# Cross attention's first keys, two blocks' queries and the first block's maxima made beside self attention's last pair of heads

## The reference, cut to what matters

```python
x = x + attn(layernorm(x))             # 16 heads of 16, causal, ALiBi
q = (layernorm(x) @ Wq + bq)           # cross attention: (2048, 16 heads, 64)
k = (ctx @ Wk + bk); v = (ctx @ Wv + bv)   # (1601, 16 heads, 64)
scores = einsum('bqhd,bkhd->bhqk', q, k) / 8
out = einsum('bhqk,bkhd->bqhd', softmax(scores), v) @ Wo + bo + layernorm(x)
x = x + layernorm(out) * gamma + beta
x = x + fp8_product(layernorm(x))
```

## Time and profile before

| | us |
|---|---|
| median of 3 runs | 1922.67 |
| lowest, highest | 1912.9, 1936.35 |
| profiled execution, its own time | 1929.99 |
| its span, first to last instruction | 1928.2 |
| PE busy, mean granted clock | 1758.9, 0.947 |
| DVE / ACT / POOL busy | 1289.3 / 921.8 / 974.3 |

### The profile page before, as it was taken

The page is one execution under the profiler, slowest core; times in us unless marked ns, Lnnn a source line. Parts: engine busy times, 40 slices in busy tenths (PEclk is TensorE's granted clock), DMA queues, the critical chain, the costliest instruction groups (busy, mean ns, idle before and its releaser), DMA issues.

```text
span 1928.2 us, 29741 instructions
## 1 busy us (share of the span) xinstructions
PE 1758.9 (91%) x10650; PEld 886.1 (46%) x10650; DVE 1289.3 (67%) x2503; ACT 921.8 (48%) x1866; POOL 974.3 (51%) x824
## 2 busy tenths in 40 slices
PE   7989988988998999999999999999999999999962
PEld 3544444434444544445545545545544554554421
DVE  5677777766733557756756655665665665678998
ACT  2346667656765243244444444445445445445531
POOL 1000000000001466558888888898898898882244
PEclk9879999889988899899999999999999999999985
DMA  4232311250011000000000000000000000000001
GB/s 115 35 36 36 35 18 19 36 98 2 1 47 42 11 0 1 1 11 4 1 10 4 1 10 4 1 11 1 4 10 1 4 1 1 4 11 23 1 28 38
DMA packets 29129, 34.48 MB, mean 18 GB/s; under 512 B 4290, under 2 KB 27139, under 8 KB 27523
## 3 DMA queue, kind: packets, MB, share of 16 engines
q1 hardware_dynamic: 28984, 32.59, 9.1%
HBM read 14.99 MB, written 4.19 MB: 10 GB/s over the span
## 4 chain that ended last, share of the span: by engine, by line
PE 76%; DVE 16%; issue 3%; ACT 3%; SPq 1%; POOL 1%; DMA 0%; POOLq 0%; ACTq 0%; DVEq 0%
PE psum L964 17%; PE psum L944 14%; PE psum L929 9%; DVE maxima L1229 8%; PE psum L850 7%; PE psum L762 6%; PE psum L800 4%; PE psum L825 4%; PE psum L987 3%; PE psum L917 3%; PE psum L862 2%; PE psum L975 2%; DVE parts_room L1323 1%; DVE stack_room L1279 1%; PE psum L877 1%
## 5 line engine op out<-in xcount | busy, mean ns | idle before, releaser
L1229 DVE TENSOR_REDUCE maxima<-psum 128x1 f32<-128x400 f32 (+5 forms) x1664 | 858.8, 578 | 315.2 <-PE psum L929 214.3
L737 POOL TENSOR_TENSOR parts_room<-parts_room,weights_room 128x512 f32<-128x512 f32 (+1 forms) x565 | 705.6, 1279 | 141.3 <-ACT weights_room L1119 141.3
L1119 ACT ACTIVATE weights_room<-psum 128x512 f32<-128x512 f32 (+1 forms) x757 | 405.8, 599 | 500.2 <-PE psum L944 423.4
L1047 ACT ACTIVATE weights_room<-psum 128x512 f32<-128x512 f32 (+3 forms) x640 | 300.1, 534 | 178.1 <-PE psum L825 99.5
L1436 POOL TENSOR_SCALAR rstd<-meanvar 128x2 f32<-128x2 f32 (+1 forms) x24 | 8.2, 343 | 650.7 <-DVE meanvar L1179 650.7
L944 PE MATMUL psum<-stack_room,dk_hi 64*128 64x512 f32 (+1 forms) x1408 | 264.5, 410 | 4.9 <-ACT weights_room L1119 4.8
L929 PE MATMUL psum<-k_later,stack_room 64*128 64x400 f32 (+1 forms) x896 | 243.6, 412 | 22.5 <-DVE stack_room L1279 14.6
L929 PEld LDWEIGHTS psum<-k_later,stack_room 64*128 64x128 f32 x896 | 129.0, 185 | 221.2 <-issue 121.9
L964 PE MATMUL psum<-weights_room,parts_room 128*64 128x512 f32 (+1 forms) x754 | 204.6, 610 | 0.0
L964 PE MATMUL psum<-weights_room,late_room 128*64 128x512 f32 (+1 forms) x760 | 203.9, 609 | 0.0
L825 PE MATMUL psum<-stack_room,stack_room 51*128 51x512 f32 (+3 forms) x640 | 140.1, 437 | 36.6 <-DVE maxima L1229 34.4
(11 more groups left out here) (133 smaller groups left out, 1907.7 us busy)
## 6 DMA issues: line engine op xcount, KB each, us to landing
stack_room<-parts_room SPq DMA_DIRECT2D x84, 128.0 KB
x_block<-x_dram SPq DMA_DIRECT2D x8, 512.0 KB, 4.7
x_middle<-x_block SPq DMA_DIRECT2D x4, 512.0 KB, 3.2
x_block<-x_middle SPq DMA_DIRECT2D x4, 512.0 KB, 3.8
out_dram<-x_block SPq DMA_DIRECT2D x8, 256.0 KB, 2.1
stack_room<-parts_room SPq DMA_DIRECT2D x24, 64.0 KB
parts_room<-ctx_dram SPq DMA_DIRECT2D x1, 1536.0 KB
stack_room<-shift_rows SPq DMA_DIRECT2D x64, 2.0 KB
```

The costliest lines, as they stand in the source:

```text
L737: engine.tensor_tensor(sum_[:kw, :], old[:kw, :], weights[u % NP_WEIGHTS][:kw, :], ALU.add) \
L1047: engine.activation(w_self[s % NW][:, m, 0:n], bank_of(use + m)[:, 0:n], ACT.Exp, scale=SELF_SCALE).then_inc(emptied(use + m), 1)
L1119: engine.activation(weights[u % NP_WEIGHTS][:kw, :], pair_scores[u % NSCORES][:kw, :], ACT.Exp, scale=CROSS_SCALE).then_inc(pair_exp, 1)
L1229: engine.tensor_reduce(maxima[:, p % 2, i // TB, n, i % TB, ch:ch + 1], bank_of(use + n)[:, 0:real - k0], AX.X, ALU.max) \
```

## The change

Pair 0's keys, without their rests, are made beside blocks 0 to 2 of self attention's last pair, and beside its block 3, from the tenth of its 24 steps on, the transposed residual of blocks 0 and 1, the queries of blocks 0 and 1, and the 16 chunks of block 0 with their negated maximum. `check_turned` asserts in the planner that self attention's block 2 has been turned by then. Only the rows and the key rests stand at `cross_start`. The residual and queries of blocks 2 and 3 and the residual's bias go beside block 0 of cross attention's second sweep, pair 1's keys and queries from beside block 0 to beside block 1. The waits follow: ACT's copies of keys and queries no longer wait for the end of self attention, those of the rests now do; the pads of the keys' buffers are cleared ahead of the last pair; `shifts` gets another place, and the first keys one in the room of the ALiBi table.

```diff
--- before.py
+++ after.py
@@ -173,7 +173,12 @@ class Order
     def self_turn(self, b):
         for c in range(DC):
             self.put("self_turn", b, c, banks=1)
+        self.turned = b
         self.after(OUT_LAG, lambda: self.self_out(b))
+
+    def check_turned(self, b):
+
+        assert self.turned >= b
...
-    def pair_sweep1(self, p, blocks=range(NB), waits=False):
+    def pair_sweep1(self, p, blocks=range(NB), waits=False, rows=True):
...
             made.append((len(steps) + ROWS_LAG, lambda b=b: self.put("pair_rows", p, b, banks=1)))
+        if not rows:
+            return steps
...
-    def pair_keys(self, p):
+    def pair_keys(self, p, rests=True):
         steps = []
         for b in range(NK):
             steps.append((1, lambda b=b: self.put("project_keys", p, b, banks=1)))
+            if not rests:
+                steps.append((0, lambda b=b: self.put("key_steps", p, b)))
+                continue
...
+    def resid_turn(self, b):
+        return [(1, lambda c=c: self.put("resid_turn", b, c, banks=1)) for c in range(DC)]
...
@@ -372,25 +385,31 @@ def build
             else:
-                self.interleave(self.sweep2(p), [])
+
+
+                main = self.sweep2(p)
+                last = [n for n, m in enumerate(main) if m[2] == NB - 1]
+                put("key_pads")
+                self.spread(main[:last[0]], self.pair_keys(0, rests=False), range(TB, last[0]))
+                queries = self.pair_queries(0)
+                early = self.resid_turn(0) + queries[:1] \
+                    + self.mingled(self.pair_sweep1(0, [0], rows=False), self.resid_turn(1) + queries[1:2])
+                self.spread(main[last[0]:], [(0, lambda: self.check_turned(HT))] + early, range(9, len(last)))
         while self.pending or self.soon:
             self.values()
 
-        def now(steps):
-            for _, step in steps:
-                step()
-
+        put("pair_rows", 0, 0, banks=1)
         put("cross_start")
         self.step = 0
-        now(self.pair_keys(0))
-        for b in range(NB):
-            for c in range(DC):
-                put("resid_turn", b, c, banks=1)
-        put("resid_bias")
-        now(self.pair_queries(0) + self.pair_sweep1(0, [0], waits=True))
-
-        sides = [self.pair_tiles(0) + self.pair_sweep1(0, [1]) + self.pair_keys(1) + self.pair_queries(1),
-                 self.pair_sweep1(0, [2]) + self.pair_sweep1(1, [0]), self.pair_sweep1(0, [3]) + self.pair_sweep1(1, [1]),
+        for b in range(NK):
+            put("key_rests", 0, b)
+        late = [step for b in range(HT, NB) for step in self.resid_turn(b)] + queries[HT:] \
+            + [(0, lambda: put("resid_bias"))]
+
+        rows = [(0, lambda: put("pair_rows", 0, 1, banks=1))]
+        sides = [self.pair_tiles(0) + self.pair_sweep1(0, [1], rows=False) + late[:HT] + rows + late[HT:],
+                 self.pair_sweep1(0, [2]) + self.pair_keys(1) + self.pair_queries(1) + self.pair_sweep1(1, [0]),
+                 self.pair_sweep1(0, [3]) + self.pair_sweep1(1, [1]),
                  self.mingled(self.pair_sweep1(1, [2, 3]), self.pair_tiles(1))]
...
@@ -649,13 +671,15 @@ SBUF
+
     late_room = Room(nc, sb, "late_room", NS * P * 4)
+    assert late_room.first >= slopes_at[0] and late_room.first + late_room.size <= slopes_at[1]
+    shifts = sb("shifts", [P, NB, BQ], F32R)
...
-    shifts = sb("shifts", [P, NB, BQ], F32R)
...
@@ -923,7 +947,7 @@ TensorE, pair_chunk
-                pe.wait_ge(shifts_cleared, 1)
+                pe.wait_ge(pads_cleared, 1)
...
@@ -1078,11 +1102,13 @@ ScalarE, project_keys and project_queries
                 if p >= 2:
                     act.wait_ge(pair_scored, pair_last(p - 2))
+                elif kind == "project_queries":
+
+                    act.wait_ge(*scores_made(last_step(NP - HP + p, NB - 1)))
                 else:
 
-                    act.wait_ge(*scores_made(SELF_STEPS - 1))
-                    act.wait_ge(values_done, SELF_STEPS)
-                    act.wait_ge(*bank_filled(use_of["self_project", NB - 1, 1]))
+                    for c in range(DC):
+                        act.wait_ge(*bank_filled(use_of["context_turn", -(-S // BQ) - 1, c]))
...
@@ -1101,6 +1127,12 @@ ScalarE, key_rests
                 act.wait_ge(*bank_read(use_of["project_keys", p, b]))
+                if p >= 2:
+                    act.wait_ge(pair_scored, pair_last(p - 2))
+                else:
+
+                    act.wait_ge(values_done, SELF_STEPS)
+                    act.wait_ge(*bank_filled(use_of["self_project", NB - 1, 1]))
...
@@ -1436,15 +1468,18 @@ GpSimd
+            elif kind == "key_pads":
+
+                for c in range(DC):
+                    pool.wait_ge(*bank_filled(use_of["context_turn", -(-S // BQ) - 1, c]))
+                chain.on(engine.memset(k_later[:, S:SE].bitcast(F32), 0.0))
+                after_last()
+                engine.memset(k_first[:, S:SE].bitcast(F32), 0.0).then_inc(pads_cleared, 1)
             elif kind == "cross_start":
...
-                for k in (k_first, k_later):
-                    chain.on(engine.memset(k[:, S:SE].bitcast(F32), 0.0))
-                    after_last()
                 engine.memset(shifts[:, :, :].bitcast(F32), 0.0).then_inc(shifts_cleared, 1)

```

11 lines of the change are left out of this document (7 added, 4 removed).

## The result

| | before | after |
|---|---|---|
| median (us) | 1919.25 (4 runs) | 1947.72 (4 runs) |
| lowest, highest | 1912.9, 1936.35 | 1939.9, 1953.08 |
| profiled execution, its own time | 1929.99 | 1953.08 |
| its span, mean granted clock | 1928.2, 0.947 | 1951.3, 0.937 |

The ratio on record is 1.0117 with a 95% interval of 1.0064 to 1.0169; the two medians alone would give 1.0148. The change makes the kernel slower by over 1%. The forecast was 1919, the range 1903 to 1936, and slower had a chance of 0.07. The prediction was wrong.

A forecast was written before the change was run, and what follows sets the result against it. PE, busy 91% of the span, was taken as the bound, so gains come from its waits or low clock. -33.0 + 5.5 + 15.5 + 6.3 + 2.0 = -3.7 us on 1922.67 gave 1919, range 1903 to 1936.

The forecast's parts named there:

- Step 3: Block 3 of self attention's last pair: added turns, queries and 16 chunks cost +15.5 us, bounds +11.0 to +20.
- step 2: Blocks 0 to 2 of self attention's last pair: pair 0's keys cost +5.5 us, bounds +1.6 and +11.
- sign of being wrong: Wrong if the last pair grows under 15 or over 30 us, or both cross blocks' sum by over 10.
- stop of about 4 us behind the normalisation: Block 3 of the last pair: maxima queue behind block 2's normalisation on DVE, PE stands some 4 us.
- Step 4: First two cross blocks: two residual blocks and two queries added, +6.3 us; bounds +1.3 and +9.3.
- step 5: SP's queue: pair 2's loads stand ahead of block 1's rows, so PE waits; +2.0 us, bounds +0.2 and +4.
- Step 1: Stretch after self attention: first cross scores about 9.4 us behind the last projection instead of 42.4; -33.0 us.
- the 5 us stand: Before the first cross scores: PE stands still some 5 us behind the first value tiles, with nothing charged for its clock.
- the clock rival: Block 3 of the last pair: its mixed stretch runs at 1.2 GHz, +15.1 us, total 1934; chance 0.13.

The follow-up runs named there:

- e1: The kernel before, unedited, run again as its own control; median 1924.26 us, ratio 0.9994.
- e2: The changed kernel, unedited, run again; median 1943.51 us, ratio to the kernel before 1.0116.
- e5: The kernel before with only pair 0's keys, without rests, moved beside blocks 0 to 2 of self attention's last pair; 1937.15 us, ratio 1.0051.
- e10: The changed kernel with block 2's normalisation ten places later, just ahead of the last fold's work on DVE; 1940.46 us, ratio to before 1.0031.
- e13: The changed kernel with block 2's normalisation behind the last turn, where DVE waits for the last projection; 1938.27 us, ratio to before 1.0045.
- e14: The changed kernel with the edits of e12, e13 and e3, pair 2's load behind the rows; 1921.30 us, ratio to before 0.9950.
- e9: The changed kernel with the 32 maxima of pair 0's first block reading a quarter of their columns; 1943.11 us, ratio to before 1.0043.
- e3: The changed kernel with pair 1's keys and queries back beside cross attention's first block; 1935.72 us, ratio to before 1.0063.
- e12: The changed kernel with `shifts` cleared and `one_row` cast early, key rests and rows right behind the last fold; 1934.59 us, ratio to before 1.0003.
- e15: e7 with e12's start, normalisations of blocks 1 and 2 behind the next turn, block 0's turn three places later; 1908.77 us, ratio to before 0.9899.
- e7: The changed kernel with moved work spread wider over the last pair, pair 1's keys and queries back in the first cross block; 1931.36 us, ratio 1.0042.

## Why the prediction was wrong

**Step 3 failed in size, step 2 with it, and the forecast with them.** The prediction's own sign of being wrong came true: the last pair (A) grew by 34.8 us between e1 and e2, over its limit of 30. Step 2 put the keys beside blocks 0 to 2 at +5.5; e1 to e2 shows 40.2 to 49.9, +9.7 (e5: +8.0), inside the bound of 11 that I had kept for "all at the lower clock". Of the 9.7, 6.1 are the keys, 1.2 more idle time and 2.4 lower clock (PE busy 34.87 and 43.42). The third keys' difference waits on DVE for ACT's copies (4.17 us idle until 588.26), block 0's normalisation follows behind it, and block 1's output behind that, for which PE waits 2.52 us at 594.08. The thought that keys would fill holes was wrong by its sign: they stood ahead of what PE was to wait for next.

Step 3 put block 3 at +15.5, bounds 11 to 20; it was +25.1 (18.9 to 44.0), outside both. By the windows of e1 and after, idle time went from 1.3 to 8.5 us (+7.2), and PE's busy time from 17.6 to 35.4 (+17.9), of which 11.0 are the work counted and 6.9 the same work at a lower clock. The forecast of 15.5 was the same 11.0 of work and 4.5 of waiting, with nothing for the clock. So the term that failed is the clock in block 3, put at nothing and measured at 6.9 us, and behind it 2.7 us of waiting. I had the work right, and the stop of about 4 us behind the normalisation (4.22) right in place and size.

Where the 6.9 us stand: by the granted clock some 3.4 in the first 10.6 us (0.68), before any chunk, and some 2.8 in the 6 us from 638.00 behind the stop (0.53). e10, e13 and e14 take the stop away and have 6.0 us of 33.4 back, 2.0 of them clock. The first part begins behind block 2's fold, for which PE waits 1.28 us; e14 has the same low part without the later stop, and e1 the same wait (1.28) without the low part. So what lowers the clock there isn't shown. Of the other waits, the first chunk's for its `q_lo` (1.13 us) stood in the row before as well (1.19); the query's for its turn's copies (1.18) did not, because there eight turns stood ahead of it. My sentence that DVE's time sets the block was wrong in its measure: e9 takes 9.5 us of it away and block 3 gains 3.9.

**Step 4, the first two cross blocks.** +6.3 forecast, and +2.0 for the wait of step 5; +10.5 with that wait in e2 (C -5.8, D +16.3), and 12.7 in the middle of the eight profiles of its group (106.2 for e1's 93.5). The second block is 60.0 for "about 59", the first 44.0 for "about 42", but the second block of the kernel before at a better clock is 43.7 and not the 46.2 that I took from one execution. e3 shows how to have 3.7 to 5.9 of it back (100.3 for 104.0 and 106.2): not to move pair 1's keys and queries at all.

**Step 1 was right, and a chain that it left out ended beside its own.** From the last projection's end to the first scores 42.4 us became 9.44 (656.59 + 3.69 = 660.28 to 669.72), for 9.4 forecast; B fell by 31.5. POOL's chain ended 9.25 us behind the projection (669.53), as priced. DVE's ended 0.08 us after it (669.61): its normalisation takes 4.97 us beside POOL's work, with the cast of `one_row` behind. The prediction had no term for that chain, and that it changed nothing is luck. I had called the 5 us stand (6.59 measured) a price already in the sum. It was, yet it was also avoidable, and e12 shows that it was worth 7 us.

**Step 5 was right.** SP issues pair 2's loads just ahead of the rows, and PE waits 1.34 us for the rows at 714.26 (1.51 in e2); +2.0 forecast, +0.2 to +4 its bounds.

**The rivals.** Nearest came the clock rival (1934, chance 0.13), with a place that was right and a size too small: it was priced instead of the waits, not on top of them. The measured sizes of all steps give -31.5 + 9.7 + 25.1 + 10.5 = +13.8 for the stretch; the rest of the difference between the medians goes with a lower mean clock, for which I had no term. The row that the prediction gave for the rival does not bear it: the projection that took 6.72 us behind waits of 0.81 and 0.77 took 3.69 in e1 and in after behind waits as long. The Trainium skill, "TensorE: Matmul & The Clock Gate", section "HAM oscillation — how this bites in real kernels", was quoted for such waits; the runs agree: the 6 us behind the 4.2 us stop are at 0.53, and 6.0 us went with it.

**Where the expected gain went.** The row before had 5.0 us of idle PE in 40.9 and a clock of 0.79, which at two levels is half rate for 42% of it, 8.6 us lost (an estimate from its window in e1). By that, only these 13.6 us could be gained; the other 27 were PE's work and had to be done elsewhere. The change did that work behind new waits, and in block 3 at 0.84 where 1.00 had been. With these gone (e15) the same idea gains 20.1 us on A + B against e1 (88.7 for 108.8) and gives 6.6 back on C + D (100.1 for 93.5), where the later turns and queries went: 13.5.

**What stays open.** Why the mean clock over the whole kernel was lower by 0.006 in e2 isn't settled. The second block (D), which was at its shortest in e2's profile, and a slower part ahead of the mark may both have a share. Against e1, e15's profile is 11.8 us shorter over the whole stretch, while its ratio stands for some 19 us; the difference isn't accounted for. e9 and e10, with 2.4 and 2.7 us less in A + B, have ratios 0.7% and 0.9% under e2's, which ran on another chip than they; so ratios of different jobs can be compared to some 0.5% only, and part of what e12 and e13 show beyond their stretches may be that. How much of e15's gain over e7 belongs to each of its edits was not tried.

## What to carry to other kernels

Before moving work into an earlier stretch, split the place that it leaves into PE's own work, idle time and lost clock: only the last two can be won, and what remains may have been the cover of a latency chain, or may have kept two engines apart (e5). Move the chain with the work, or end it early: clear buffers, cast constants and make small rests where their engine is idle, and put a piece like a normalisation, which has another engine's answer inside, where its engine waits anyway. Price a stop of PE at more than its length where it is dense on both sides (4.2 us cost 6.0), and don't read a term off one execution whose clock may be 5 us off. Before a difference is put down to an edit, split it at the place where the edit begins: of the 7.6 us of e10, 1.6 stood ahead of it.

## What the runs showed of the hardware

- DVE and POOL hold each other up unevenly: four 128x256 fp32 operations of DVE took 1.38 us alone and 4.97 us beside POOL's memset and two-input operations, while POOL's took 1.80 and 3.14 us beside them, 1.80 and 3.00 alone. It was 4.97 or 4.98 us in all ten profiles in which they met, and 2.94 in e1, where the memset fell on it and the rests came later. DVE's piece ends (669.37) just as POOL's does (669.53). The Trainium skill, "SBUF — State Buffer", section "Who interferes with whom", says that the two share a port pair that one holds for a whole instruction while the other is blocked; the trace agrees, and adds that with instructions back to back on both sides the loser was DVE each time.
- The clock of one execution moves a mark behind nearly the same 540 us of work by up to 20 us (538.6 to 559.1 in seventeen profiles), and makes the same projection 3.69 or 6.16 us long.
- A stop of 4.22 us of PE in a dense stretch was followed by 6 us at a granted clock of 0.53, and the stretch was 6.0 us longer with it than without (33.3 to 33.4 us in five profiles, 27.3 in three).
